# The order of a prologue's Gram products, remainders and first norm, and of one group's load and remainder behind the loop

## The reference

```python
dx = x[:, 1:] - x[:, :-1]                      # steps of the path
sig = path_signature(dx, depth=4)              # running levels of 8, 64, 512, 4096 terms
h = sig @ W.T + b                              # 4680 -> 128
h = h + attention(layernorm(h))                # 8 heads of 64, own token masked, spectral-normed weights
h = h + moe(layernorm(h)) + shared(layernorm(h))  # 8 experts, top 1, hidden 512; shared: gelu, hidden 512
def spectral_norm(W, u, sigma):                # for w_qkv (1536 x 128) and w_out (128 x 512)
    v = W @ u / norm(W @ u); u2 = W.T @ v / norm(W.T @ v)
    return W / (v @ W @ u2) * sigma
```

## Time and profile before

| | us |
|---|---|
| median of 3 runs | 646.62 |
| all runs | 649.11, 646.62, 646.20 |
| the profiled execution | 645.78 |
| its span in the profile | 644.0 |
| TensorE busy | 617.4 (96%) |
| VectorE busy | 428.9 (67%) |
| GpSimd busy | 321.4 (50%) |
| ScalarE busy | 290.1 (45%) |
| mean granted clock of TensorE | 0.988 |

### The profile page before, as it was taken

The page is one execution under the profiler, slowest core; times in us unless marked ns, Lnnn a source line. Parts: engine busy times, 40 slices in busy tenths (PEclk is TensorE's granted clock), DMA queues, the critical chain, the costliest instruction groups (busy, mean ns, idle before and its releaser), DMA issues.

```text
span 644.0 us, 13364 instructions
## 1 busy us (share of the span) xinstructions
PE 617.4 (96%) x4085; PEld 519.6 (81%) x4085; DVE 428.9 (67%) x1093; ACT 290.1 (45%) x640; POOL 321.4 (50%) x336
## 2 busy tenths in 40 slices
PE   5989999999999999999999999999989999999993
PEld 3767888887888887888888787888768899999992
DVE  6976777766777766777776778788556535666450
ACT  4324444444344455344444444444464545666331
POOL 2455544454554455554455455445854501566663
PEclk9989999999999999999999999999999999999997
DMA  8611443345553334343334434111235712444330
GB/s 302 247 76 34 100 98 82 82 102 110 101 128 82 82 86 119 89 104 92 82 82 111 102 94 103 38 37 39 69 98 176 203 49 62 55 54 56 43 47 2
DMA packets 69902, 59.80 MB, mean 93 GB/s; under 512 B 6513, under 2 KB 58609, under 8 KB 69489
## 3 DMA queue, kind: packets, MB, share of 16 engines
q1 hardware_dynamic: 63232, 55.21, 33.2%
q0 software_dynamic: 6640, 4.22, 4.9%
HBM read 16.79 MB, written 26.30 MB: 67 GB/s over the span
## 4 chain that ended last, share of the span: by engine, by line
PE 83%; DVE 8%; POOL 3%; issue 3%; ACT 1%; DMA 0%; SPq 0%; ACTq 0%; DVEq 0%; POOLq 0%
PE bank L1300 77%; PE bank L1511 2%; PE bank L1356 2%; POOL z L492 1%; POOL sorted_rows L507 1%; DVE z L921 1%; PE bank L1611 1%; PE bank L1405 1%; POOL z L494 1%; PE bank L1360 0%; PE bank L1414 0%; DVE mask L1104 0%; DMA h<-x_prev 0%; POOL rstd L501 0%; DVE rowmax L1046 0%
## 5 line engine op out<-in xcount | busy, mean ns | idle before, releaser
L1300 PE MATMUL bank<-whigh,uth 128*128 128x512 f32 x512 | 168.2, 409 | 1.2 <-DVE lowt L815 1.2
L1300 PEld LDWEIGHTS bank<-whigh,uth 128*128 128x128 f32 x512 | 92.4, 190 | 26.8 <-issue 7.5
L1300 PE MATMUL bank<-whigh,utl 128*128 128x512 f32 x256 | 101.9, 398 | 0.0
L581 POOL DMA_INDIRECT out<-xvo,ids x39 | 61.3, 1572 | 65.0 <-ACT xvo L770 58.1
L501 POOL TENSOR_TENSOR rstd<-rstd,powers 128x1 f32<-128x1 f32 x64 | 35.2, 550 | 113.9 <-DVE rstd L908 65.9
L492 POOL TENSOR_TENSOR z<-z 128x512 f32<-128x512 f32 x32 | 42.2, 1319 | 70.6 <-DVE z L921 70.6
L1300 PE MATMUL bank<-xT,qkw 128*128 128x128 f32 x512 | 63.4, 277 | 0.0
L656 ACT ACTIVATE prob<-prob 128x512 f32<-128x512 f32 x32 | 20.2, 633 | 93.3 <-DVE prob L1048 93.3
L1300 PEld LDWEIGHTS bank<-xT,qkw 128*128 128x128 f32 x512 | 59.6, 192 | 0.7 <-issue 0.4
L1300 PEld LDWEIGHTS bank<-whigh,utl 128*128 128x128 f32 x256 | 48.4, 189 | 11.4
L487 POOL TENSOR_TENSOR e3l<-e,e3h 128x512 fp32r<-128x512 f32 x31 | 41.1, 1325 | 26.9 <-DVE xn L942 26.4
(11 more groups left out here) (236 smaller groups left out, 1357.8 us busy)
## 6 DMA issues: line engine op xcount, KB each, us to landing
sorted_rows<-blank SPq DMA_DIRECT2D x24, 709.5 KB, 5.9
xvp<-xvo SPq DMA_DIRECT2D x128, 128.0 KB, 2.3
w<-w_t SPq DMA_DIRECT2D x1, 4096.0 KB, 12.0
w<-w_high SPq DMA_DIRECT2D x4, 512.0 KB, 6.5
x_columns<-x2t SPq DMA_DIRECT2D x32, 64.0 KB, 1.6
xg_in<-x_columns SPq DMA_DIRECT2D x8, 256.0 KB, 5.6
levels<-w_t SPq DMA_DIRECT2D x1, 2048.0 KB, 8.8
out<-h SPq DMA_DIRECT2D x8, 256.0 KB, 2.2
```

The costliest lines, as they stand in the source:

```text
L581: nc.gpsimd.indirect_dma_start(out=out[:, :], out_offset=bass.IndirectOffsetOnAxis(ap=ids[:, tile:tile + 1], axis=0), in_=y[:, 2 if j == S ...
L1300: return T.matmul(out_, lhsT, rhs, start=start, stop=stop)
```

## The change

It moves instructions and removes none. On TensorE the 12 products of `gram_qkv` are issued in pieces of 3, 2 and 7, the first two around `sum_level3(0)`; `project(1, ...)` is cut elsewhere, so that three chunks stand ahead of `accumulate(0)` and three between the product of `gram_out` and `x_columns(0)`. On VectorE `signature_lo(0)` goes behind `features_lo(0)`, `features_lo(1)` ahead of the large `low_outer`, the copies of `gram_out` and `wu_out` ahead of `first_norm(0)`, and `add_s2(1)` between `first_norm(0)` and its finish. Behind the loop, `load_group(4)` goes ahead of `spill(31)`, w2's load behind `load_group(6)`, and `x_group_lo(4, 0)` ahead of `add_shared(0, 0)` and the slot counts; VectorE's loop over the groups is written out, in the same order otherwise.

```diff
@@ -419,8 +419,9 @@
             sp.wait_ge(xg_lo, 2)
             load_group(3)
             spill(TILES - 2)
+            sp.wait_ge(xg_lo, 3)
+            load_group(4)
             spill(TILES - 1)
-            sp.dma_start(w2, w2_t).then_inc(ld_w2, 16)
             sp.wait_ge(x2T_sent, 16 * TILES)
 
             def load_rows(j, k):
@@ -432,9 +433,11 @@
                     .then_inc(rows_in[k], 16)
 
             for g in range(GROUPS):
-                if g + 4 < GROUPS:
+                if 0 < g and g + 4 < GROUPS:
                     sp.wait_ge(xg_lo, g + 3)
                     load_group(g + 4)
+                if g == 2:
+                    sp.dma_start(w2, w2_t).then_inc(ld_w2, 16)
                 sp.wait_ge(added, g + 1)
                 sp.dma_start(out[g * GROUP * P:(g + 1) * GROUP * P, :].rearrange("(t p) d -> p t d", p=P),
                              h[:, g * GROUP:(g + 1) * GROUP, :]).then_inc(out_sent[g], 16)
@@ -890,7 +893,6 @@
             level4(0)
             level2(2)
             level2(3)
-            signature_lo(0)
 
             def one(ap):
                 return ap.rearrange("p o c -> p (o c)")
@@ -1088,6 +1090,7 @@
                 return n_norm
 
             features_lo(0)
+            signature_lo(0)
             d.wait_ge(ld_sn, 48)
             d.wait_ge(norm_mm, 1)
             made = nstep(V.tensor_tensor(gram_u, B[5][:, 0:DIM], uq[:], ALU.mult))
@@ -1110,18 +1113,17 @@
             d.wait_ge(consts_cast, 2)
             weigh(0, 0, True)
             weigh(0, 1)
+            features_lo(1)
             rest_made = low_outer(slice(per, TILES))
-            features_lo(1)
-            first_norm(0)
-            first_norm_finish(0)
-            after(rest_made)
-            made = add_s2(1)
-            assert made == SECOND_GROUP_STEPS
-
             d.wait_ge(norm_mm, 2)
             V.tensor_copy(gram_out, B[5][:, 0:DIM])
             made = nstep(V.tensor_copy(wu_out[:], B[5][:, DIM:DIM + 1]))
             assert made == OUT_COLUMN_STEP
+            first_norm(0)
+            after(rest_made)
+            made = add_s2(1)
+            assert made == SECOND_GROUP_STEPS
+            first_norm_finish(0)
             V.tensor_tensor(nrm[:, 0:1], ucol[:, 0:1], wtwu[:], ALU.mult)
             V.tensor_tensor(nrm[:, 1:2], wtwu[:], wtwu[:], ALU.mult)
             V.tensor_tensor(nrm[:, 2:3], wu_out[:], wu_out[:], ALU.mult)
@@ -1179,6 +1181,7 @@
             te_bank = [B[n][:, 0:rest * EXPERTS].rearrange("p (t e) -> p t e", e=EXPERTS) for n in (4, 7)]
             running(slice(EARLY, TILES), te_bank[1], tot, incl, 1)
             place(slice(EARLY, TILES), te_bank[0], oh, pick, tot, incl, pos_f, 1)
+            x_group_lo(4, 0)
             add_shared(0, 0)
 
             (count, ntiles, pairs, end_p, gap_p, room, taken, following, rest_, end_r, gap_r) = (
@@ -1224,10 +1227,10 @@
             V.tensor_copy(row_i[:], row_f[:]).then_inc(pos_ready, 1)
             assert n_route == ROUTE_STEPS
 
-            with d.Fori(2, GROUPS - 3, 2) as g:
-                for k in range(2):
-                    x_group_lo(g + (k + 2), k)
-                    add_shared(g + (k - 1), 1 - k)
+            for g in range(1, GROUPS - 3):
+                add_shared(g, g % 2)
+                if g + 4 < GROUPS:
+                    x_group_lo(g + 4, g % 2)
             def expert_weights(j):
 
                 k = j % 2
@@ -1326,12 +1329,13 @@
                         if c == PAIRS - 1:
                             last.then_inc(ww_psum, 1)
 
-            def gram_qkv():
+            def gram_qkv(lo, hi):
 
                 nq = 3 * INNER // P
-                for c in range(nq):
+                for c in range(lo, hi):
                     last = mm(B[5][:, 0:DIM], wqkv_sb[:, c, :], wqkv_sb[:, c, :], c == 0, c == nq - 1)
-                last.then_inc(norm_mm, 1)
+                if hi == nq:
+                    last.then_inc(norm_mm, 1)
 
             def gram_wout():
 
@@ -1537,11 +1541,13 @@
             sum_level2(0)
             pe.wait_ge(ld_w, 16)
             weight_products(B[6:8], PAIRS, wqkv_sb[:, 0:PAIRS, :])
+            gram_qkv(0, 3)
             pe.wait_ge(before_cast, 1)
             sum_level3(0)
+            gram_qkv(3, 5)
             pe.wait_ge(ld_sq, 32)
             features(0, False)
-            gram_qkv()
+            gram_qkv(5, 3 * INNER // P)
             project_first_hi(0)
             sum_level3(1)
             pe.wait_ge(ld_wo, 16)
@@ -1557,14 +1563,15 @@
             pe.wait_ge(ww_lo, 2)
             sum_level2(3)
             gram_wout()
-            project(1, 0, 1)
+            project(1, 0, 3)
             accumulate(0)
-            project(1, 1, UC + 1)
+            project(1, 3, UC + 1)
             pe.wait_ge(norm_step, OUT_COLUMN_STEP)
             mm(B[5][:, DIM + 1:DIM + 2], gram_out, wu_out[:]).then_inc(norm_mm, 1)
+            project(1, UC + 1, 8)
             x_columns(0)
             sum_level3(2)
-            project(1, UC + 1, 9)
+            project(1, 8, 9)
             pe.wait_ge(small, SECOND_GROUP_STEPS)
             pe.wait_ge(norm_step, SUMS_STEP)
             mm(B[6][:, 256:260], ones, nrm[:]).then_inc(norm_mm, 1)
```

## The result

The changed kernel takes 641.65 us in the median of 4 runs (641.37 to 641.93); the kernel before, with one more run beside it, 647.12 us (646.20 to 649.11). The ratio is 0.991 (95% interval 0.989 to 0.994): 0.9% faster, where 0.6% was forecast. (The 641.65 us by itself is not; the kernel before came out 0.5 us longer beside it.) The two profiled executions alone, 645.78 and 641.93 us, differ by 3.85 us, which is the forecast's 3.8. So there are two things to explain: where the 3.85 us came from, and why the medians are another 1.1 to 1.6 us apart (5.5 us here, 4.9 in a repeat further down).

What follows compares the result with a forecast made beforehand. TensorE bounds the loop, VectorE's chain the prologue up to accumulate(1) at 48.82. Prologue 2.45 plus tail 1.37 make 3.8 us: profiled 645.78 becomes 642.0, median 646.62 becomes 642.8 us; range 641.4 to 643.5, with rivals to 644.8.

Steps and rivals of the forecast that it cites:

- (a): Prologue: Gram products in pieces, signature_lo(0) behind features_lo(0); VectorE's chain moves up by 0.6 us.
- (b): Prologue: features_lo(1) ahead of low_outer; z1 comes at 33.75 instead of 34.3, 0.55 us gained, bounds 0 and 1.15.
- (b), TensorE's wait: Prologue: TensorE's 1.21 us wait for the remainder of the second tile's features goes.
- the half clock at 35 us: Prologue: granted clock 0.52 there, judged worth little by itself, since TensorE waited for wu_out at its end even so.
- (c): Prologue: Gram copies ahead of first_norm run in VectorE's idle time before h; 0.4 us off the chain.
- (d): Prologue: add_s2(1) goes into VectorE's gap after rstd; 1.2 us leave the chain behind it.
- (e): Prologue: VectorE's 0.29 us wait for the sums before the reciprocal goes; 0.3 us.
- Behind the loop, 1.37 us: Near 504 us: earlier load and remainder of group 4 end TensorE's wait; gain 1.37 us, bounds 0.9 and 1.4.
- the 0.4 us that were left for down(2, 0): Behind the loop: add_shared(0, 0) ends at 499.55, down(2, 0) asks for it at 499.99.
- the spare time of group 7: Behind the loop: group 7 lands about 517, remainder wanted at 522.9; 5.9 us less 1.5 for cast and remainder spare.
- The rivals: Clock falls in pauses 644.0 us, 14%; chain gain eaten 644.7, 12%; tail gains nothing 644.2, 7%; slower 650.6, 4%.
- the signs of being wrong: z1 of tile 0 no earlier than 34.3, granted clock falling between 38 and 48 us, group 7's remainder after 522.

Runs made afterwards that it cites:

- a repeat further down: The changed kernel timed again beside the kernel before, in another group: 641.23 us, ratio 0.9922.
- parts_cd_only: The kernel before with only the gram_out and wu_out copies ahead of first_norm(0) and add_s2(1) ahead of its finish: 645.98 us, ratio 0.9991.
- part_b_only: The kernel before with only features_lo(1) ahead of low_outer and three chunks of project(1, ...) ahead of accumulate(0): 648.45 us, ratio 1.0028.
- tail_remainder_only: The kernel before with only group 4's remainder ahead of add_shared(0, 0), the loads left where they were: 652.51 us, ratio 1.0082.
- part_a_only: The kernel before with only the Gram products in pieces and signature_lo(0) behind features_lo(0): 645.73 us, ratio 0.9992.
- tail_only: The kernel before with only group 4's load, w2's load and group 4's remainder moved, prologue as before: 644.84 us, ratio 0.9973.

## Why the prediction was off

**What bounds the kernel**: right for the profiled execution. VectorE's chain sets accumulate(1), and behind it only 0.3 us more came up in the loop's last tiles (2.34 us at the last x2 columns).

**(a) 0.6 us, and (b)'s 0.55 us from z1**: this is the term that was mis-sized, and the two are one. The 0.55 us is 34.3 less 33.75, and 33.75 stands on weigh(0, 1) ending 0.6 us earlier, at 29.55. From that end to z1 the working had 4.20 us; the trace shows 4.17 (30.00 to 34.17), and 4.14 in the kernel before. So the stall was worked out right, (b)'s new order brought z1 nothing, and what could reach h was (a)'s gain alone. In the profiled pair that was 0.15 us at weigh(0, 1) and 0.04 at h. VectorE's chain started 0.28 us later there (16.26 instead of 15.98, in part behind a level-3 sum at 12.16 that was slow in that execution), and from features_lo(0) to the Gram product it took 2.6 us where I had 2.4. That the Gram product is no longer waited for is right. But the size of that wait was taken from one execution, 0.57 us. In two others of the same code it is 0.93 and 1.65 us. Counted from VectorE's first product, h comes after 30.97 and 30.75 us in the two profiles of the changed kernel, so the term of 0.55 us is 0.1 to 0.3 us against the profiled execution of before, and 0.8 to 1.75 us against the other two.

**(b), TensorE's wait**: its true worth was named and put aside, in "the half clock at 35 us is worth little by itself". That is so while VectorE's chain is as long as before (13.96 to 14.01 us from h to accumulate(1), with the fall or without). Shortened by (c) and (d), the chain waits for TensorE (1.57 us in parts_cd_only), so the change's gain rests on (b) keeping TensorE going: 0.95 us in the profiles. The sum lost nothing by it, since it assumed that TensorE keeps up.

**(c), (d), (e)**: 0.4, 1.2 and 0.3 us forecast, 1.96 measured together between h (34.86 to 34.82) and the reciprocal (43.32 to 41.32). Right, in the changed kernel, where (b) keeps TensorE in time.

**Behind the loop, 1.37 us**: 1.62 in the profile, 1.7 by the medians. Right, as were the 0.4 us that were left for down(2, 0); the spare time of group 7 was there too, 3 us instead of the 4.4 worked out.

**The sum and the range**: for the profiled pair the 3.8 us came out (3.85), with some luck: 0.4 us less in the prologue, 0.25 more behind the loop and 0.3 in the loop's last tiles cancel. The step that failed is to carry this sum to the median by adding 0.84 us, with the Gram product's wait at its size in one short execution. The kernel before took 645.4 to 649.1 us in all its runs, and the profiled 645.78 us is among its short ones; the changed kernel's runs lie within 0.6 us of one another in either group. Against the median the prologue gave 3.4 us for the 2.45 forecast, and the whole 5.0 to 5.8 us by the two ratios (0.9922 and 0.9911) for the 3.8. The low end of the range, 641.4 us, is the profiled 645.78 less both upper bounds, 3.0 and 1.4; it has no room for executions that start otherwise. The upper end, 643.5, follows from neither starting point (646.62 less 1.9 and 0.9 is 643.8). It was a near miss: by the repeat's ratio the changed kernel is at 641.6 us, just inside.

**The rivals**: none came. The clock didn't fall in the pauses of 1.34 and 1.00 us that the change makes; in part_b_only and tail_remainder_only it fell behind pauses of 3.40 and 4.27 us. Of the signs of being wrong, z1 of tile 0 came close: 34.17, against 34.3. What stays open is what else than the Gram block lengthens the longer executions of the kernel before: part (a) alone removes VectorE's wait, and yet gives 0.4 us and keeps the spread.

## What to carry to other kernels

When two engines are nearly level in a stretch, take parts of an edit together: here one part alone cost 1.8 us, the others gave about half a microsecond each, hardly clear of noise, and all three gave 3.4. A pause of TensorE that is off the path can put it on the path, through the clock at which it runs afterwards, and the same pause need not do so in every execution. And before a sum is set against a profile, look at where the profiled execution lies in the spread of the runs: a wait for TensorE's first block can be three times as long in another execution, and an edit that ends it is then worth more than the profile shows. Look for VectorE and GpSimd instructions that are twice as long as their like; here they pointed to another 1.7 to 2.4 us.

## What the runs showed of the hardware

The granted clock's column read 1.00 from the start to the first recorded fall, also where passes took the time of the lower level: 0.77 us for a pass of 128x512 in tail_only against 0.47 in the profiled execution of before, with the column at 1.00 in both. In the changed kernel two passes of one kind take 2.08 us at 6.85 and 1.13 us at 28.86, again at 1.00 in both. The durations of like passes, not that column, tell at which clock a start ran. By the column alone, the shorter executions of the kernel before look like the ones with the lower clock (0.988 against 0.994).

A GpSimd add of 256 columns took 2.20 us beside a VectorE product of two SBUF operands, and 0.73 without; a VectorE cast of 512 columns 2.75 us beside GpSimd's product, and 0.41 without.

Falls of the granted clock to 0.50 stood behind pauses of TensorE of 1.10 (before, at 14 us), 1.21, 1.22, 1.39, 3.40 and 4.27 us. Pauses of 1.22 (tail_remainder_only) and 1.39 us (part_a_only) at the same place in the program, and of 2.01 us ahead of wu_out's product in both, were followed by none. The length of the pause alone does not tell.
